# First attention layer: scores of the next batch directly behind the values, normalised rows on ACT, another order of projections and banks

## The chip, the cores and the metric

The kernel runs on one core of one Trainium2 chip. The metric is the device time of one execution in microseconds, as the median of several runs. The profile comes from one further execution that the hardware profiler recorded. The engines are PE (TensorE: matmuls; PEld is its weight load), DVE (VectorE), ACT (ScalarE), POOL (GpSimd) and SP (SyncE, which here only issues DMAs). Each engine works through its own instructions in order; semaphores order them against each other. PSUM has eight banks, which PE alone fills with products and DVE and ACT read.

## What is computed

x is 32 batches of 128 rows of 128 features; the context is 32 x 77 x 128. Two layers follow each other, each a cross-attention and a feed-forward part, with a layer norm ahead of each part and a residual behind it. The change touches only the attention of the first layer:

```python
x = x + _L0_xattn_ref(_layernorm(x, axis=-1), ctx_1024, ctx_1024, L0_xattn_Wq, ..., L0_xattn_Wo, mask_BxSxS2_ik0)
...
Q = (q @ Wq).reshape(b, ql, N_HEAD, QK_DIM)      # 16 heads of 64
K = (k @ Wk).reshape(b, kl, N_HEAD, QK_DIM)
V = (v @ Wv).reshape(b, kl, N_HEAD, V_DIM)
Q, K = (rope(Q), rope(K))
attn = jnp.einsum('bqhd,bkhd->bhqk', Q / scale, K)
attn = jnp.where(mask[:, None, :, :] == 0, -INF, attn)
attn = jax.nn.softmax(attn, axis=-1)
out = jnp.einsum('bhqk,bkhd->bqhd', attn, V).reshape(b, ql, N_HEAD * V_DIM)
return out @ Wo
```

## The kernel before

Every engine's program of this layer is a loop over 32 slots, one for each batch b, written out in full; a pair p = b // 2 of batches shares one set of queries, and j = b % 2 tells the even from the odd slot. Keys are projected for quads of four batches in eight tasks `("K", n)`, values in five tiles of 128 context rows for eight batches (`("V", u, half)`), queries of the next pair in four tasks `("Q", p + 1, k)`, and the turned normalised rows of the pair after it in one task `("X", p + 2)`.

In a slot PE does this for batch b: `all_scores` (L1274: 32 float32 products that make the scores with the keys as rows, in three banks `ps` and one bank `pa`; L1278: 16 bfloat16 products, the folds, that add mask and row maximum from the tile `fold`), `values` (L1296: probabilities times values), `turn_out` (L1307: the normalised output is transposed), `out_projection` (L1316). For batch b + 1 it does `score_maxima` (L1223 lays the mask into `ps`, L1232 adds bfloat16 scores with the queries as rows; DVE takes the row maxima of them at L911 and writes them into `am`) and `turn_maxima` (L1244: `am` is transposed into `ps[0]`; ACT copies it into `fold` in `fold_in`, L1057). Projections are split products of three fp32r matmuls each (L1172 to L1174). PE transposes `xhat` at L1164.

DVE ropes the query and key tasks out of their bank (L845, L848 for queries; L855, L858 for keys; the second one frees the bank), POOL finishes the rope (L741, L742, L753, L755), ACT casts the result to bfloat16 for the maxima (`cast_queries` L1045, `cast_keys` L1053). ACT also takes the exponents (`exps`, L1062 for the group in `pa`, L1067 for those in `ps`), copies the values out of their bank (`values_in`, L1040) and the transposed output (`turned_out`, L1073). DVE normalises the output (`normalise`, L917 to L924), adds the residual (L929), and makes the rows of the pair p + 2: `statistics`, `masks` (L801, L802) and `normalised_rows` (L817: a 128x2 scale; L819: two 128x128 steps), which write `xhat`.

The projections, the turned rows and one group of scores share the two banks `pa[0]` and `pa[1]`. `pa_tasks` lists them in PE's order and `TASK` deals them out in turn: each task takes the bank that the last but one had, and PE waits until that one's reader has freed it. `TASK` sets no order itself; PE's order is the one in which `slot` is written. `VALUE_SLOT` and `KEYS` say which slot projects what. In all the text below, a slot of kind A is b = 4q, B is 4q + 1, C is 4q + 2 and D is 4q + 3. The layer's scores begin at 30 us and its last slots end at about 440 us. In layer 1, L1788 is an ACT `Identity` with a bias, which stands in one loop with exponents (L1812).

Of the kernel before, what the change touches and what calls it, by code (L numbers as in the profile page):

```python
# [403 lines left out]
def layer0_attention(nc, ctx, t):  # L404
# [64 lines left out]
    setup = sem("setup")  # L469
    stats_ready, rstd_ready, xhat_ready = sem("stats_ready"), sem("rstd_ready"), sem("xhat_ready")  # L470
# [14 lines left out]
    VALUE_SLOT = {8 * o + s: VT * o + i for o in range(B // 8) for i, s in enumerate((-3, 0 if o == 0 else -1, 1, 3, 4))  # L485
                  if 8 * o + s >= 0}
# [3 lines left out]
    KEYS, LATE_KEYS = {0: range(4, 8), 1: range(8, 11), 2: range(14, 16)}, {1: range(11, 14)}  # L490
    for q in range(1, B // 4 - 1):
        n = 8 + 8 * q
        KEYS[4 * q], KEYS[4 * q + 1], LATE_KEYS[4 * q + 1] = range(n, n + 2), range(n + 2, n + 5), range(n + 5, n + 7)
        KEYS[4 * q + 2] = range(n + 7, n + 8)

    def middle_keys(b):

        return KEYS[0][:2] if b == 0 else ()

    def even_keys(b):  # L500

        return KEYS.get(b, ())[2 if b == 0 else 0:]

    def odd_keys(b):

        return KEYS.get(b, ())[:2], KEYS.get(b, ())[2:]

    def late_keys(b):

        return LATE_KEYS.get(b, ())  # L510

    def pa_tasks():

        yield from ([("X", 0)] + [("Q", 0, k) for k in range(4)] + [("V", 0, 0)] + [("K", n) for n in range(4)]
                    + [("V", 0, 1), ("C",), ("X", 1)])
        for b in range(B):
            p, u = b // 2, VALUE_SLOT.get(b)
            values = [] if u is None else [("V", u, 0), ("V", u, 1)]
            tasks = lambda ns: [("K", n) for n in ns]
            queries = [("Q", p + 1, k) for k in range(4)] if p + 1 < PAIRS else []  # L520
            if b < B - 2:
                yield "S", b
            if b % 2 == 0:
                yield from (queries[:2] + tasks(middle_keys(b)) + queries[2:3] + tasks(even_keys(b)[:-1]) + queries[3:] + values
                            + tasks(even_keys(b)[-1:]))
                continue
            ahead, behind = odd_keys(b)
            rows = [("X", p + 2)] if p + 2 < PAIRS else []
            if ahead:
                yield from tasks(ahead) + rows + tasks(behind) + values + tasks(late_keys(b))  # L530
            else:
                yield from values[:1] + rows + values[1:]
# [1883 lines left out]
```

## Time and profile before

| | us |
|---|---|
| median of 3 runs | 718.12 |
| the runs | 717.88, 718.12, 720.57 |
| the profiled execution | 719.26 |
| its span, first to last instruction | 716.7 |

| engine | busy us | share of the span |
|---|---|---|
| PE | 680.4 | 95% |
| PEld | 569.8 | 80% |
| DVE | 556.9 | 78% |
| POOL | 432.1 | 60% |
| ACT | 388.7 | 54% |

The page gives the share of busy time of each engine, the granted clock of PE (0.995 of full speed over the span, so the higher of its two levels, 2.4 GHz, nearly throughout), and the instructions by group. PE's matmuls are pipelined: a row of a single one shows some 0.2 to 0.5 us, while the next begins long before that ends. So the time that a matmul costs is the distance from its start to the next start, and a short wait can hide within the duration of the one before it without a gap.

### The profile page before, as it was taken

The numbers are of one execution on the slowest core, as the hardware profiler recorded it, in microseconds if no ns is written. First come the engines' busy times: TensorE is split into PE (matmuls) and PEld (weight loads), VectorE is DVE, ScalarE is ACT, GpSimd is POOL, SyncE is SP. The second block draws the span as 40 slices with busy tenths as digits, with TensorE's granted clock in tenths as the row PEclk, the third lists the DMA queues.
The fourth block names the chain that finished last, engine by engine and source line by source line (L and its number), as shares of the span: only waits on it lengthen the run. The fifth ranks groups of instructions, "written<-read, shape, count | busy, mean of one in ns | idle before, by whom it ended". The sixth has DMA issues, their size and how long they took to land.

```text
span 716.7 us, 23519 instructions
## 1 busy us (share of the span) xinstructions
PE 680.4 (95%) x9268; PEld 569.8 (80%) x9273; DVE 556.9 (78%) x1635; ACT 388.7 (54%) x846; POOL 432.1 (60%) x558
## 2 busy tenths in 40 slices
PE   8999999999999999999999989999999999998875
PEld 6788888888888888889888878788888888875544
DVE  5887787697687698688687655787878887778996
ACT  2443553543544544445345444566766766766896
POOL 3597586487396388378477523455555646632775
PEclk9999999999999999999999999999999999998999
DMA  9511011101101101101100120000000000000011
GB/s 263 132 34 37 13 48 45 33 5 46 37 26 45 36 2 45 36 26 36 36 22 15 32 79 7 11 7 7 12 5 4 9 4 9 0 2 1 24 45 52
DMA packets 26766, 23.82 MB, mean 33 GB/s; under 512 B 7148, under 2 KB 23356, under 8 KB 26680
## 3 DMA queue, kind: packets, MB, share of 16 engines
q1 hardware_dynamic: 25864, 22.25, 11.1%
q8 instruction: 62, 1.02, 0.6%
q10 hardware_dynamic: 816, 0.36, 0.2%
q14 instruction: 24, 0.20, 0.1%
HBM read 10.25 MB, written 2.10 MB: 17 GB/s over the span
## 4 chain that ended last, share of the span: by engine, by line
PE 70%; DVE 17%; POOL 5%; issue 4%; ACT 3%; DMA 1%; SPq 0%; ACTq 0%; DVEq 0%
PE bank L1274 7%; PE bank L1316 6%; PE bank L1942 6%; PE bank L1172 5%; PE bank L1296 4%; PE bank L1975 4%; PE bank L1278 4%; PE bank L1307 3%; PE bank L1173 3%; PE bank L1174 3%; DVE a_am L911 3%; PE bank L1960 2%; DVE f_h_max L2192 2%; PE bank L1223 2%; PE bank L1232 2%
## 5 line engine op out<-in xcount | busy, mean ns | idle before, releaser
L741 POOL TENSOR_TENSOR a_turned<-a_turned,a_rope 128x512 f32<-128x512 f32 x63 | 81.7, 1297 | 55.7 <-DVE a_turned L848 55.7
L742 POOL TENSOR_TENSOR a_qr<-a_straight,a_turned 128x512 f32<-128x512 f32 x64 | 81.6, 1276 | 4.9
L845 DVE TENSOR_TENSOR a_straight<-bank,a_rope 128x512 f32<-128x512 f32 x63 | 43.0, 683 | 52.5 <-PE bank L1174 51.4
L1045 ACT CAST a_qb<-a_qr 128x512 bf16<-128x512 f32 x64 | 39.8, 622 | 65.9 <-POOL a_qr L742 65.9
L1296 PE MATMUL bank<-a_vs,a_probs 77*64 77x65 f32 x2048 | 66.8, 222 | 0.0
L1296 PEld LDWEIGHTS bank<-a_vs,a_probs 77*64 77x64 f32 x2048 | 62.6, 137 | 3.3
L753 POOL TENSOR_TENSOR a_k_turned<-a_k_turned,a_rope 128x308 f32<-128x308 f32 x61 | 48.4, 793 | 24.3 <-DVE a_k_turned L858 23.6
L1316 PE MATMUL bank<-a_wo,a_oTn 128*128 128x128 f32 x512 | 62.6, 275 | 0.2 <-ACT a_oTn L1073 0.2
L1316 PEld LDWEIGHTS bank<-a_wo,a_oTn 128*128 128x128 f32 x512 | 60.5, 192 | 1.2 <-ACT a_oTn L1073 0.5
L911 DVE TENSOR_REDUCE a_am<-bank 128x6 bf16<-128x462 f32 (+1 forms) x96 | 49.9, 576 | 12.1 <-PE bank L1232 12.0
L1274 PE MATMUL bank<-a_qr,a_kr 64*77 64x128 f32 x960 | 59.2, 273 | 0.0
L1057 ACT COPY a_fold<-bank 112x128 bf16<-112x128 bf16 x32 | 8.5, 266 | 92.4 <-PE bank L1244 92.4
L1067 ACT ACTIVATE a_probs<-bank 77x512 f32<-77x512 f32 x98 | 52.8, 593 | 7.5 <-PE bank L1258 7.5
L1274 PEld LDWEIGHTS bank<-a_qr,a_kr 64*77 64x77 f32 x960 | 52.3, 144 | 5.2 <-issue 5.1
L755 POOL TENSOR_TENSOR a_kr<-a_k_straight,a_k_turned 128x308 f32<-128x308 f32 x62 | 52.0, 840 | 4.8
L848 DVE STREAM_SHUFFLE a_turned<-bank 128x512 f32<-128x512 f32 x63 | 46.3, 735 | 0.0
L1674 DVE TENSOR_REDUCE a_max_m<-bank 128x8 f32<-128x512 f32 x64 | 41.1, 685 | 5.0 <-PE bank L1923 4.6
L1812 ACT ACTIVATE a_qr<-bank 128x512 f32<-128x512 f32 (+1 forms) x96 | 43.8, 536 | 1.0 <-PE bank L1960 1.0
L729 POOL TENSOR_TENSOR a_rstd<-a_var,minus_half 128x2 f32<-128x2 f32 x16 | 11.3, 707 | 51.1 <-DVE a_var L812 51.0
L1073 ACT COPY a_oTn<-bank 128x512 f32<-128x512 f32 x64 | 34.5, 589 | 13.4 <-PE bank L1307 12.8
L1172 PE MATMUL bank<-a_xT_hi,a_wq_hi 128*128 128x256 f32 x128 | 39.9, 312 | 1.3 <-DVE a_wq_lo L939 1.1
L1599 POOL TENSOR_TENSOR a_kr<-a_k_straight,a_blocks 128x128 f32<-128x128 f32 x32 | 12.8, 400 | 46.4 <-ACT a_k_straight L1794 46.4
(282 smaller groups left out, 1984.8 us busy)
## 6 DMA issues: line engine op xcount, KB each, us to landing
a_vs<-a_stage SPq DMA_DIRECT2D x16, 312.8 KB
out<-x_all SPq DMA_DIRECT2D x16, 128.0 KB, 1.8
x_all<-in_x_dram SPq DMA_DIRECT2D x7, 256.0 KB, 6.3
a_vs<-a_stage SPq DMA_DIRECT2D x4, 308.8 KB
a_mask_in<-in_mask SPq DMA_DIRECT2D x16, 77.0 KB, 5.7
a_wv<-in_ctx SPq DMA_DIRECT2D x16, 77.0 KB
a_ctx_in<-in_ctx SPq DMA_DIRECT2D x8, 128.0 KB
a_vs<-a_stage SPq DMA_DIRECT2D x4, 211.2 KB
```

The source lines that it names most:

```text
L741: steps.link(nc.gpsimd.tensor_tensor(tv, tv, rope[:, 1:2, :].broadcast_to([128, 4, S]), ALU.mult))
L742: nc.gpsimd.tensor_tensor(qr[P][:, 2 * k:2 * k + 2, :, :].rearrange("p t j s -> p (t j) s"), sv, tv, ALU.subtract if made else ALU.add).th ...
L753: steps.link(nc.gpsimd.tensor_tensor(tv, tv, rope[:, 3:4, 0:KL].broadcast_to([128, 4, KL]), ALU.mult))
L755: nc.gpsimd.tensor_tensor(kr[q % 2][:, lo:hi, first:end, :].rearrange("p i j s -> p i (j s)"), view(k_straight[n % 3]), view(k_turned[n % ...
L848: nc.vector.stream_shuffle(turned[k % 3][:], pv, mask=[lane ^ 1 for lane in range(32)]).then_inc(a_free[TASK["Q", p, k][0]], 1)
L911: nc.vector.tensor_reduce(rows, ps[bk][:, 0:n * KL].rearrange("p (h k) -> p h k", k=KL), AX, ALU.max).then_inc(s_free[bk], 1)
L1067: nc.scalar.activation(probs[:, 4 * g:4 * g + 4, :], ps[ST_BANK[g]][0:KL, :].rearrange("p (h s) -> p h s", s=S), ACT.Exp).then_inc(s_free[ ...
L1172: nc.tensor.matmul(out, lhs_hi, rhs_hi, start=True, stop=False)
L1274: nc.tensor.matmul(banks[g][0:KL, i * S:(i + 1) * S], kr[b // 4 % 2][e:e + 64, h // 2, b % 4, :], qr[P][e:e + 64, h // 2, j, :], start=i = ...
L1296: last = nc.tensor.matmul(po[r][rows, VW * i:VW * (i + 1)], probs[:, PROBS_SLOT[h], rows], vs[b % RING][:, h, :], start=True, stop=True)
L1316: last = nc.tensor.matmul(po[2][:, 0:D], oTn[:, i, :], wo[:, i, :], start=i == 0, stop=i == TILES - 1)
L1812: nc.scalar.activation(probs[:, 4 * g:4 * g + n, :], SCORES[g].rearrange("p (t s) -> p t s", s=S), ACT.Exp).then_inc(s_free[g], 1)
```

## The change

- The scores of batch b + 1 (the L1274 part, without the folds) are written directly behind `values(b)`, ahead of `turn_maxima(b + 1)` and `turn_out(b)`; the slot of b + 1 then begins with the folds (`all_folds`). For batches 0 to 29.
- `turn_maxima` writes a bank `pa` (a new task `("T", b)`) in place of `ps[0]`.
- `turned_out(b)` on ACT stands at the end of slot b in place of the next slot's start or middle; ACT's exponents of a slot are no longer divided by it.
- `normalised_rows` of pairs 2 and up is four ACT steps in the even slot in place of three DVE steps in the odd one: two centre the rows, two scale them. The scale is made on POOL (one 128x2 product behind the power). What it needs of the mask comes from `mask_in` itself, with two DVE steps ahead of the statistics.
- PE's order of the projections and `pa_tasks` change: one key task stands directly behind the folds in A, B and C (`lead`), two in B; the first value tile stands in the middle of the slot between keys. `VALUE_SLOT` moves tile 0 of eight batches from slot 8o - 3 to 8o - 1, and tile 4 from 8o + 4 to 8o + 5.
- `score_maxima` lays the mask before it waits for the keys' cast, and waits for the queries' casts too.
- SP loads the mask of pair 2 before the later loads, and each further one a slot earlier.

The core of the diff:

```diff
-    VALUE_SLOT = {8 * o + s: VT * o + i for o in range(B // 8) for i, s in enumerate((-3, 0 if o == 0 else -1, 1, 3, 4))
-                  if 8 * o + s >= 0}
+    VALUE_SLOT = {0: (1,), **{8 * o + 1: (VT * o + 2,) for o in range(B // 8)}, **{8 * o + 3: (VT * o + 3,) for o in range(B // 8)},
+                  **{8 * o + 5: (VT * o + 4,) for o in range(B // 8)},
+                  **{8 * o - 1: (VT * o, VT * o + 1) for o in range(1, B // 8)}}
...
     def statistics(p):
+            if p > 1:
+                dve.wait_ge(xhat_ready, p)
+                dve.wait_ge(masks_in[p % 2], 16 * (p // 2) + 16)
+                steps.link(nc.vector.tensor_reduce(kept[p % 2][:], mask_in[p % 2][:], AX, ALU.max, apply_absolute_value=True))
+                steps.did(nc.vector.tensor_scalar(kept[p % 2][:], kept[p % 2][:], 0.5, -1.0, ALU.is_ge, ALU.mult))
...
     def scalar(act, second):
+        def normalised_rows(p):
+            act.wait_ge(rstd_ready, p + 1)
+            for j in range(2):
+                nc.scalar.activation(xhat[:, j, :], x[:, 2 * p + j, :], ACT.Identity, bias=mv[p % 2][:, j, 0:1],
+                                     scale=-1.0).then_inc(rows_centred, 1)
+            for j in range(2):
+                act.wait_ge(rows_centred, 2 * (p - 2) + j + 1)
+                last = nc.scalar.activation(xhat[:, j, :], xhat[:, j, :], ACT.Identity, scale=scale[:, j:j + 1])
+            last.then_inc(xhat_ready, 1)
...
+                exps(b, (3, 0, 1, 2))
+                if j == 0:
+                    if more_pre(p):
+                        normalised_rows(p + 2)
+                    cast_keys(b + 1)
...
+                fold_in(b + 1)
+                if b + 1 < B - 2:
+                    turned_out(b, 0)
+                    turned_out(b, 1)
...
         def score_maxima(b, P, j):
-            pe.wait_ge(cast_done, b + 1)
+            pe.wait_ge(masks_made, b // 2 + 1)
             for m in (2, 0, 1):
...
+            pe.wait_ge(cast_done, b + 1)
+            pe.wait_ge(queries_cast, Q_GROUPS * (b // 2 + 1))
...
         def turn_maxima(b, P, j):
...
+            if b < B - 2:
+                nc.tensor.transpose(empty(pe, ("T", b))[:].bitcast(BF16)[0:FOLD, 0:S], am[P][:, j, :],
+                                    t["identb"][:]).then_inc(a_full[TASK["T", b][0]], 1)
+                return
...
+        def all_folds(b):
+            pe.wait_ge(a_free[TASK["T", b][0]], TASK["T", b][1] + 1)
...
             elif j == 0:
-                all_scores(b, P, j)
+                all_folds(b)
+                for n in lead:
+                    project_keys(n)
+                project_queries(p + 1, (0,))
+                if not first:
+                    out_projection(b - 1)
+                project_queries(p + 1, (1,))
...
                 for r in range(3):
                     values(b, P, j, r)
+                all_scores(b + 1, P, 1)
                 turn_maxima(b + 1, P, 1)
-                if u is not None:
-                    project_values(u, 0)
-                    project_values(u, 1)
-                for n in even_keys(b)[-1:]:
-                    project_keys(n)
+                turn_out(b)
```

PE from the end of the values of batch 1 (slot B) into the next slot, before: the maxima are turned, a value tile and three key tasks follow, then `turn_out(1)` and the scores with their folds.

```order
L1296 MATMUL bank<-a_vs,a_probs 64x65 x7
L1244 MATMUL bank<-identb,a_am 112x128 [waits a0_s_free0,a0_s_free2,a0_s_free1]
L1172 MATMUL bank<-a_wv_hi,a_ctxT_hi 128x512 [waits a0_a_free1]
...
L1174 MATMUL bank<-a_ctxT_hi,a_wk_lo 128x308
L1307 MATMUL bank<-ident,a_out_n 128x128 [waits a0_normalised]
L1307 MATMUL bank<-ident,a_out_n 128x128 x5
L1307 MATMUL bank<-ident,a_out_n 128x128 [waits a0_normalised]
L1307 MATMUL bank<-ident,a_out_n 128x128
L1274 MATMUL bank<-a_qr,a_kr 77x128 [waits a0_s_free1,a0_s_free2]
```

The same place now:

```order
L1342 MATMUL bank<-a_vs,a_probs 64x65 x7
L1316 MATMUL bank<-a_qr,a_kr 77x128 [waits a0_s_free1,a0_s_free2]
L1316 MATMUL bank<-a_qr,a_kr 77x128 x7
L1316 MATMUL bank<-a_qr,a_kr 77x128 [waits a0_a_free1,a0_s_free0]
L1316 MATMUL bank<-a_qr,a_kr 77x128 x7
L1283 MATMUL bank<-identb,a_am 112x128 [waits a0_s_free0,a0_a_free0,a0_s_free2,a0_s_free1]
L1353 MATMUL bank<-ident,a_out_n 128x128 [waits a0_normalised]
L1353 MATMUL bank<-ident,a_out_n 128x128 x5
L1353 MATMUL bank<-ident,a_out_n 128x128 [waits a0_normalised]
L1353 MATMUL bank<-ident,a_out_n 128x128
L1324 MATMUL bank<-a_fold,a_fold_w 77x128 [waits a0_a_free0]
```

The scores have moved ahead of the turned maxima and of `turn_out`, the value and key tasks have left this place, and the folds alone stand behind `turn_out`.

PE in the middle of slot B (batch 1), now: keys, two value halves, a key task and the turned rows follow `out_projection`, with the bank that each waits for.

```order
L1362 MATMUL bank<-a_wo,a_oTn 128x128 x3
L1208 MATMUL bank<-a_ctxT_hi,a_wk_hi 128x308 [waits a0_a_free1]
...
L1208 MATMUL bank<-a_wv_hi,a_ctxT_hi 128x512 [waits a0_a_free0,a0_a_free1]
...
L1208 MATMUL bank<-a_wv_hi,a_ctxT_hi 128x512 [waits a0_a_free1]
...
L1208 MATMUL bank<-a_ctxT_hi,a_wk_hi 128x308 [waits a0_a_free1,a0_a_free0]
...
L1200 MATMUL bank<-ident,a_xhat 128x128 [waits a0_contexts_in0,a0_a_free1,a0_xhat_ready]
```

Before, this place held the turned rows and one key task behind `out_projection`, and the value halves came behind the turned maxima.

ACT in the even slot C (batch 2), before:

```order
L1073 COPY a_oTn<-bank 128x512 [waits a0_turned_full] x2
L1053 CAST a_kb<-a_kr 128x616 [waits a0_a_free1,a0_a_free0,a0_k_roped]
L1062 ACTIVATE a_probs<-bank 77x512 [waits a0_a_full0]
L1067 ACTIVATE a_probs<-bank 77x512 [waits a0_s_full0]
L1067 ACTIVATE a_probs<-bank 77x512 [waits a0_s_full1]
L1067 ACTIVATE a_probs<-bank 77x512 [waits a0_s_full2]
L1045 CAST a_qb<-a_qr 128x512 [waits a0_roped]
```

And now:

```order
L1103 COPY a_oTn<-bank 128x512 [waits a0_turned_full] x2
L1092 ACTIVATE a_probs<-bank 77x512 [waits a0_a_full1]
L1097 ACTIVATE a_probs<-bank 77x512 [waits a0_s_full0]
L1097 ACTIVATE a_probs<-bank 77x512 [waits a0_s_full1]
L1097 ACTIVATE a_probs<-bank 77x512 [waits a0_s_full2]
L1043 ACTIVATE a_xhat<-x_all,a_mv 128x128 [waits a0_rstd_ready]
L1043 ACTIVATE a_xhat<-x_all,a_mv 128x128
L1047 ACTIVATE a_xhat<-a_xhat,a_scale 128x128 [waits a0_rows_centred] x2
L1080 CAST a_kb<-a_kr 128x616 [waits a0_a_free1,a0_a_free0,a0_k_roped]
L1072 CAST a_qb<-a_qr 128x512 [waits a0_roped]
```

The four steps of the rows have come in behind the exponents, and the cast of the keys, for which `score_maxima` waits, has moved from ahead of the exponents to behind the rows.

## Rows read from the trace of the kernel before

**Rows 1.** The steady stretch: bounds; length; busy PE, PEld, DVE, ACT, POOL; clock; DMA.
```profile
48.00:420.00 372.00, 362.62 (x5142) 316.87 (x5139) 283.62 (x737) 174.23 (x350) 244.20 (x242) 1.00 0.12 34
```

**Rows 2.** PE's waits, 48 to 420 us: waiting, releaser, total, times, longest.
```profile
PE bank L1164 <- DVE a_k_turned L858: 2.0, 3, 0.7
PE bank L1244 <- DVE a_am L911: 1.7, 4, 0.4
PE bank L1307 <- DVE a_out_n L918: 1.4, 6, 0.3
```

**Rows 3.** Timeline of PE at four waits: start, length, instruction, idle time before.
```profile
155.89 1.95 PE L1316 MATMUL bank<-a_wo,a_oTn 128*128 128x128 f32 x16
158.52 0.41 PE L1164 MATMUL bank<-ident,a_xhat 128*128 128x128 f32 x2 [0.68 <-DVE a_k_turned L858]
...
216.58 0.40 PE L1174 MATMUL bank<-a_wv_hi,a_ctxT_lo 128*128 128x512 f32 x1
217.04 0.38 PE L1172 MATMUL bank<-a_ctxT_hi,a_wk_hi 128*128 128x308 f32 x1
...
217.40 0.31 PE L1174 MATMUL bank<-a_ctxT_hi,a_wk_lo 128*128 128x308 f32 x1
217.75 0.38 PE L1172 MATMUL bank<-a_ctxT_hi,a_wk_hi 128*128 128x308 f32 x1
...
241.18 0.40 PE L1174 MATMUL bank<-a_wv_hi,a_ctxT_lo 128*128 128x512 f32 x1
241.83 1.09 PE L1307 MATMUL bank<-ident,a_out_n 128*128 128x128 f32 x8 [0.26 <-DVE a_out_n L918]
```

**Rows 4.** Timeline of PE where it waits for nothing: its price by starts.
```profile
216.11 0.40 PE L1172 MATMUL bank<-a_wv_hi,a_ctxT_hi 128*128 128x512 f32 x1
...
221.13 1.09 PE L1278 MATMUL bank<-a_fold,a_fold_w 112*77 112x128 bf16 x16
222.02 0.36 PE L1172 MATMUL bank<-a_xT_hi,a_wq_hi 128*128 128x256 f32 x1
...
223.54 1.95 PE L1316 MATMUL bank<-a_wo,a_oTn 128*128 128x128 f32 x16
225.24 0.36 PE L1172 MATMUL bank<-a_xT_hi,a_wq_hi 128*128 128x256 f32 x1
```

**Rows 5.** Timeline of ACT and PE around `turn_out` and the next folds.
```profile
242.52 1.07 ACT L1073 COPY a_oTn<-bank 128x512 f32<-128x512 f32 x2 [0.33 <-PE bank L1307]
243.48 0.72 ACT L1053 CAST a_kb<-a_kr 128x616 bf16<-128x616 f32 x1
245.21 0.59 ACT L1062 ACTIVATE a_probs<-bank 77x512 f32<-77x512 f32 x1 [1.01 <-PE bank L1278]
245.71 1.55 ACT L1067 ACTIVATE a_probs<-bank 77x512 f32<-77x512 f32 x3
...
244.76 1.09 PE L1278 MATMUL bank<-a_fold,a_fold_w 112*77 112x128 bf16 x16
```

**Rows 6.** DVE and ACT groups: count, busy us, mean ns, idle; then one timeline row.
```profile
L819 DVE SCALAR_TENSOR_TENSOR a_xhat<-x_all,a_mv,a_scale 128x128 f32<-128x128 f32 x28 | 28.6, 1060 | 0.5
L817 DVE SCALAR_TENSOR_TENSOR a_scale<-a_kept,a_rstd 128x2 f32<-128x2 f32 x13 | 10.7, 823 | 0.4
L1788 ACT ACTIVATE a_k_straight<-bank,a_bk 128x154 f32<-128x154 f32 x16 | 6.2, 389 | 7.6 <-PE bank L1894 7.6
...
26.18 0.61 DVE L819 SCALAR_TENSOR_TENSOR a_xhat<-x_all,a_mv,a_scale 128x128 f32<-128x128 f32 x2
```

**Rows 7.** Timeline: how soon DVE and ACT free a bank.
```profile
216.31 1.29 ACT L1040 COPY a_stage<-bank 128x512 f32<-128x512 f32 x2 [0.56 <-PE bank L1174]
...
218.15 0.50 DVE L858 STREAM_SHUFFLE a_k_turned<-bank 128x308 f32<-128x308 f32 x1
```

**Rows 8.** Timeline of PE and ACT at the layer's first scores.
```profile
30.00 1.98 PE L1274 MATMUL bank<-a_qr,a_kr 64*77 64x128 f32 x32
...
30.10 0.27 ACT L1057 COPY a_fold<-bank 112x128 bf16<-112x128 bf16 x1 [0.45 <-PE bank L1244]
```

More of the change, by code:

```diff
@@ L527, in pa_tasks @@
[L527 to L530, printed above, removed]
-            else:
-                yield from values[:1] + rows + values[1:]
+            p = b // 2
+            lead, second, middle, late = ([("K", n) for n in some] for some in keys_at(b))
+            first_half, second_half = ([("V", u, half) for u in ahead_values(b)] for half in range(2))
@@ new lines, in pa_tasks @@
+            later_first, later_second = ([("V", u, half) for u in later_values(b)] for half in range(2))
+            if b % 2 == 0:
+                queries = [("Q", p + 1, k) for k in range(4)] if p + 1 < PAIRS else []
+                if b == 0:
+                    yield from (queries[:2] + first_half + middle[:1] + second_half + middle[1:] + queries[2:3] + late[:1]
+                                + queries[3:] + late[1:])
+                else:
+                    yield from lead + queries
+            else:
+                rows = [("X", p + 2)] if p + 2 < PAIRS else []
+                yield from (lead + second + middle[:1] + first_half + second_half + middle[1:] + later_first + rows
+                            + later_second + late)
@@ L766, in slot @@
         def slot(b, p, P, j, more):
+            lead, second_keys, middle, late = keys_at(b)
             if j == 0:
@@ L780, in slot @@
                     rope_turn(p + 1, 1 - P, 3)
-                for n in even_keys(b)[-1:]:
+                for n in late[1:]:
                     rope_keys(n)
             else:
-                ahead, behind = odd_keys(b)
-                for n in (*ahead, *behind, *late_keys(b)):
+                for n in (*lead, *second_keys, *middle, *late):
                     rope_keys(n)
@@ L963, in slot @@
             first = b == 0
+            lead, second_keys, middle, late = keys_at(b)
             if j == 0 and last_pair(p):
@@ L1005, in slot @@
                     next(second)
+                if more_pre(p) and lead:
+                    split_turned(("X", p + 2))
                 if more:
                     maxima(b + 1, 1 - P, 0)
-                if more_pre(p) and not ahead:
+                if more_pre(p) and not lead:
                     split_turned(("X", p + 2))
+                for n in late:
+                    rope_keys(n)
                 normalise(b)
@@ L1132, in slot @@
[L1132 to L1145 removed]
+                exps(b, (2, 3))
@@ L1351, in tensor @@
         idle_products(6)
+        all_scores(0, 0, 0)
         turn_maxima(0, 0, 0)
         def slot(b, p, P, j, more):
-            first, u = b == 0, VALUE_SLOT.get(b)
+            first = b == 0
+            lead, second_keys, middle, late = keys_at(b)
             if j == 0 and last_pair(p):
```

243 lines of the change are left out of this document (128 added, 115 removed).

## The prediction

> **What bounds the kernel now.** I read the busy times first, then the steady stretch of the first layer, then PE's waits in it, then the starts of single matmuls. The page gives PE 95% busy over the span; in the stretch from 48 to 420 us it is 362.6 of 372.0 us, DVE 283.6, POOL 244.2, ACT 174.2 [rows 1]. PE bounds the stretch. The number of its products stays the same, so the change can only take away waits of PE, or make new ones. Nothing behind the layer's last slots is touched.
>
> PE's idle time there is 372.0 - 362.6 = 9.4 us, and three of its releasers are DVE: the rows of the pair ahead (2.0 us), the row maxima (1.7), the normalised output (1.4) [rows 2]. The reader should not stop at these. A matmul's record reaches over part of the wait behind it, so I compare starts [rows 3]. Between the start of the last value product and `turn_out` lie 0.65 us where 0.23 is the price of that product (0.47 for two, from 216.11 to 216.58 [rows 3, 4]): 0.42 lost, of which the view shows 0.26. From a value tile to a key task it is 0.46 in place of 0.23, with no idle time shown, and from a key task to the next 0.35, of which I take 0.14 as the price. `out_projection` takes 1.70 us [rows 4] where nothing holds it; before the turned rows it took 2.63 (155.89 to 158.52), some 0.85 too much.
>
> Counted over the slots by their order: about 17 waits at value and key tasks for a bank, 0.22 each and all hidden (3.7 us), and some 16 others that hide about 0.15 beside what is shown (2.4). **All of PE's waits there come to 9.4 + 3.7 + 2.4 = 15.5 us.** That is the most that perfect cover could give in this stretch, 2% of the kernel.
>
> **The rows move from DVE to ACT.** DVE gives up L819 and L817, in one pair of batches 2 x 1.06 + 0.82 = 2.94 us [rows 6], and the reduction of `kept` moves rather than goes. It gains a 128x2 step. The work is in slots B and D, just ahead of where PE waits for it; afterwards it is in A and C, on ACT. That ends the wait of the turned rows (2.0 us shown), and makes key tasks and maxima in B be served sooner. The two L819 take 0.61 us together at 26.18 [rows 6], where POOL is idle, and 1.06 each on the mean beside POOL.
>
> The Trainium skill (page "SBUF — State Buffer", section "SBUF: two separate sides") says that a VectorE operation with two SBUF inputs and a GpSimd operation that reads SBUF shut each other out for a whole instruction, and that ScalarE waits for neither. The trace agrees on the first half with 0.61 against 2 x 1.06. It also speaks against a small part of this change: the new 128x2 step reads and writes SBUF in a form that would take the same lock, so that beside POOL it may wait out one POOL step. No row here shows that step.
>
> On ACT the rows cost four 128x128 steps. The nearest row is L1788, 128x154 with a bias, 0.39 us [rows 6]; below it lies about 0.3, above it 0.5 with the wait between centring and scaling. I take 0.45, so 1.8 us a pair, 1.2 to 2.4. ACT is 47% busy, so it has the room; whether it stands in anybody's way is a matter of place. In A and C the keys' cast now stands behind them. ACT starts `turned_out` 0.69 us after `turn_out` began and is done 0.96 later (241.83, 242.52, 243.48 [rows 3, 5]), so it is free 1.65 us behind that start. `turn_out` takes 0.9 to 1.0; so the first exponent can start 0.7 us into the slot, and the four take 2.05 (245.21 to 247.26 [rows 5]). The rows end at 2.8 + 1.8 = 4.6, the cast (0.6 to 0.7) at 5.3. PE needs it behind folds 0.9, key 0.5, three query tasks of 0.75, `out_projection` 1.7 and the mask's 0.65: at 6.0. Cover of 0.7 us, so I cost this at nothing; each microsecond beyond that would cost 14, once for each pair.
>
> POOL gets one more 128x2 step behind the power (about 0.8 us, an estimate from L817, the same shape on DVE [rows 6]); its 244 of 372 us hide that, and the rows are wanted only at 2.8 into the slot.
>
> **The scores move behind the values.** Two waits get cover. The scores stand 1.9 us long between the values and `turn_out`, so DVE's normalising is done when `turn_out` starts: the seven waits of 0.4 (2.8 us) go. The maxima are wanted for the scores' banks at the same place as before, so their 0.48 us waits go only as far as DVE is earlier; it is, by the 2.9 us above. Against that, the folds lose the scores as cover for `fold_in`: it starts 0.10 us behind the scores' start and takes 0.27 at the first batch [rows 8], and `turn_out` with its 0.9 us covers it in every slot but the first. There nothing does: **+0.7 us** once (one bank wait with it, 0.4 to 1.0).
>
> There is a second effect, of changes between kinds of matmul: a split product's first matmul is dearer by 0.08 behind another kind (the first two of a key task take 0.36, from 217.04 to 217.40, where 0.14 is the price of one), and a score behind a projection alike. The order has about one such change less in a slot. 28 slots by 0.08 would be -2.2; the passage from `turn_out` to the folds is in no row and may cost as much. I take **-1.0**, bounds -3 and +2.
>
> **The other order of projections.** A bank is free about 1.1 us after the last start of a key task (217.40 to 218.65, less 0.14 [rows 3, 7]), and a value half about 0.9 us after its end (ACT's 0.59 and some 0.25 ahead of it). In B the order is now key, value half, value half, key, turned rows, and every task takes the bank of the last but one. The second value half wants the bank of the key two places ahead, with only a half of 0.70 us between (0.47 for two products, so 0.70 for three [rows 3, 4]): about 0.45 lost. The turned rows want the bank of that half with only a key of 0.44 between: about 0.35 lost. So 0.8 us in each of seven slots B: **5.6 us of waits stay or are new**, 3 to 7. In A, C and D I find each bank freed in time: the query tasks are spread over `out_projection`. In A, B and C a second task directly behind the folds wants the bank of the first exponent. That is done at 0.7 + 0.6 = 1.3 us, and wanted at 0.9 + 0.44 = 1.35. I cost it at nothing, with 0.3 as the far end, in 21 slots.
>
> In slot 0, V and K tasks now stand among the first queries and wait for DVE's 1.25 us a query; by the same working 1.75 us of waits against 1.5 before: **+0.2**. In the last slots one wait for DVE stays, which no scores cover (0.7), and small ones of ACT: **1.0 stays**. Values in place, masks and the later loads: the values' tile 0 is made about a slot ahead of its use, over 10 us, and the masks come sooner than before. Both at nothing.
>
> **The sum.** 15.5 - 5.6 - 1.0 = 8.9 us of waits gone, 1.0 for the kinds, less 0.7 and 0.2: 9.0. My list surely misses a few small waits; I take 0.5 off for them. The profiled execution of 719.26 becomes 710.8. It lies 1.14 above the median of 718.12, which carries over: **709.6 us**.
>
> **The rivals.**
> 1. *The wait moves to the exponents.* The task behind the lead key waits 0.3 us in 21 slots, since ACT now does `turned_out` ahead of the exponents: 6.3 us back, 715.9. For it speaks that my cover is 0.05 us. Against it, that the exponent's 0.59 us is measured, and that `turned_out` stood ahead of the exponents in even slots before too, with no idle time of PE behind it.
> 2. *The rows on ACT hold up the maxima.* If the four steps came late (the statistics late on DVE, a step of 0.8 us and not 0.45, or a change of function between exponent and identity), the keys' cast would end beyond 6.0 us and PE would stand at `score_maxima` in 14 even slots. It decides from 0.7 us; at 1.7 us late it costs 14, less the 8.5: 723.6. Against it: L1788, an identity among exponents, takes 0.39 [rows 6].
> 3. *Nearly all waits go.* If DVE frees the banks in B quicker since nothing is queued ahead, and the order of kinds gives its 3: 15.5 - 2 + 3 less 0.9 is 15.6, so 702.5.
> 4. *Nothing happens*, since DVE is behind all along and the waits only change their names: 718. Against it, DVE's 283.6 of 372 fall by some 35.
>
> **How the numbers follow.** Forecast (705 to 713.5) 0.60; rival 1 and mixtures with it (713.5 to 717) 0.20; rival 3 0.10; rival 4 0.04; rival 2 0.06. The range 703.5 to 716.5 leaves out 2 in 10. A measurement can tell 0.5% from no change, so 714.5 and 721.7 are the bounds: faster takes the forecast, rival 3 and a part of rival 1, 0.77; same 0.17; slower 0.06.
>
> **What would show it.** In the profile after: PE 48 to 410 us with 4 to 6 us idle and not 9.4; no wait at the turned rows except in B, where the releaser is ACT's value copy and not DVE; `turn_out` directly behind the turned maxima; value half to value half in B 0.7 us apart rather than 0.23; the cast of the keys 0.5 us or more ahead of the scores of `score_maxima`. Wrong would be: gaps behind the lead key, released by the exponents (rival 1), or ahead of L1270 by ACT's cast (rival 2), or DVE's busy time not falling by some 2.5 us a pair.

## The result, and the profile after

The changed kernel takes 714.83 us (median of 20 runs, 713.07 to 716.88), the kernel before 718.71 in the same sessions (20 runs, 717.54 to 720.57). The ratio is 0.9941, 95% interval 0.9931 to 0.9952: 4.2 us faster by the ratio (3.9 by the two medians), where 8.5 were forecast. The sign and the range held, the size did not. The profiled execution took 713.36 us, its span is 711.6.

Page of the kernel after: span, busy times, and the engines of the chain that ended last.

```profile
span 711.6 us, 23628 instructions
PE 678.8 (95%) x9273; PEld 571.7 (80%) x9273; DVE 521.4 (73%) x1607; ACT 401.5 (56%) x902; POOL 435.8 (61%) x572
...
PE 83%; DVE 9%; issue 3%; ACT 3%; DMA 1%; POOL 0%; SPq 0%; ACTq 0%; DVEq 0%
```

On the page of before DVE was busy for 556.9 us and ACT for 388.7, and the chain was 70% PE and 17% DVE. DVE has lost 35 us, and half of its share of the chain.

First the stretch from 48 to 410 us (bounds; length; busy PE, PEld, DVE, ACT, POOL; clock; DMA), then PE's waits in it (waiting line, releaser, total, times, longest). In this kernel L1208 is the first product of a projection, L1200 the transpose of the rows.

```profile
48.00:410.00 362.00, 355.94 (x5070) 315.66 (x5067) 247.09 (x705) 185.27 (x401) 247.59 (x255) 1.00 0.11 31
...
PE bank L1208 <- DVE a_k_turned L874: 3.2, 8, 0.5
PE bank L1200 <- ACT a_stage L1067: 2.4, 7, 0.3
PE bank L1208 <- ACT a_probs L1092: 0.5, 1, 0.5
```

PE is idle for 6.1 us where it was 9.4 [rows 1]; up to 414 us, which is as far into the layer as 420 us in the kernel before, it is 6.1 us too. The waits for the maxima and for the normalised output are gone, and so is one that [rows 2] does not list, `score_maxima` for the cast of the keys:

```profile
PE bank L1223 <- ACT a_kb L1053: 1.8, 3, 0.9
```

The turned rows still wait, 2.4 us in seven slots where it was 2.0 in three, now for ACT's copy in place of DVE; and DVE's turned keys still release 3.2 us (2.0 and 1.1 before). What is left are banks that the order of projections asks for early. By starts, in the way of [rows 3], I count some 12 us of waits up to 414 us against the 15.5 of before: only 3 to 4 us of waits went.

The same eight slots, by the windows between the masks of `score_maxima`: before from 133.90 us, after from 134.40 us.

```profile
133.90:237.44 103.54, 101.54 (x1438) 88.92 (x1437) 81.20 (x212) 48.56 (x99) 68.79 (x68) 1.00 0.12 33
```
```profile
134.40:236.70 102.30, 100.83 (x1438) 89.32 (x1437) 70.80 (x204) 52.34 (x115) 69.79 (x72) 1.00 0.12 34
```

1.24 us less for eight slots; 10.4 us less on DVE (2.6 a pair) for 3.8 more on ACT. Between the scores of `score_maxima` of slots 4 and 28 there are 306.2 us in place of 310.5 (-4.3); the three slots behind that give 2.5 more, and the first four, to my surprise, take 1.9 away: 56.7 in place of 54.8. In both of these 0.7 us is work that has only changed its place: one value half (three matmuls) stood in slot 28 and stands among the first slots now.

**Slot B.** Timeline of PE in the B slot at 157 us (start, length, instruction, idle time before).

```profile
157.77 0.30 PE L1210 MATMUL bank<-a_ctxT_hi,a_wk_lo 128*128 128x308 f32 x1
...
158.37 0.39 PE L1210 MATMUL bank<-a_wv_hi,a_ctxT_lo 128*128 128x512 f32 x1
159.15 0.47 PE L1208 MATMUL bank<-a_wv_hi,a_ctxT_hi 128*128 128x512 f32 x1 [0.39 <-DVE a_k_turned L874]
...
160.21 0.30 PE L1210 MATMUL bank<-a_ctxT_hi,a_wk_lo 128*128 128x308 f32 x1
160.85 0.41 PE L1200 MATMUL bank<-ident,a_xhat 128*128 128x128 f32 x2 [0.34 <-ACT a_stage L1067]
...
162.82 0.30 PE L1210 MATMUL bank<-a_ctxT_hi,a_wk_lo 128*128 128x308 f32 x1
163.10 0.38 PE L1208 MATMUL bank<-a_ctxT_hi,a_wk_hi 128*128 128x308 f32 x1
```

158.37 to 159.15 is 0.78 where 0.23 is the price of the product: 0.55 lost for the middle key's bank. 160.21 to 160.85 is 0.64 where 0.14 is the price: 0.50 lost for the value half's. 162.82 to 163.10 loses another 0.14, with no idle time shown, at the second late key. Together 1.2 us in each of seven slots B (the last of them lacks the 0.14).

**The task behind the lead key.** In slot 8, as in every slot with a lead key: the first exponent on ACT, then PE's last matmul of the lead key and the first of the task behind it.

```profile
142.04 0.60 ACT L1092 ACTIVATE a_probs<-bank 77x512 f32<-77x512 f32 x1
142.55 0.30 PE L1210 MATMUL bank<-a_ctxT_hi,a_wk_lo 128*128 128x308 f32 x1
142.79 0.36 PE L1208 MATMUL bank<-a_xT_hi,a_wq_hi 128*128 128x256 f32 x1
```

142.55 to 142.79 is 0.24 where 0.14 is the price: 0.10 lost, with no idle time shown. The exponent that frees the bank ends at 142.64, and PE starts 0.15 us later. In all 20 such slots from 51 us on PE's start lies 0.14 to 0.15 us behind the end of this exponent; in 19 of them 0.10 us is lost, in slot 1 0.62. That makes 2.5 us in all.

**The first slots.** PE at the first folds, at key task 7 of slot 0, at the second key task of slot 1 and at the first query task of slot 2.

```profile
32.07 1.09 PE L1324 MATMUL bank<-a_fold,a_fold_w 112*77 112x128 bf16 x16 [0.36 <-ACT a_fold L1084]
...
44.08 0.31 PE L1208 MATMUL bank<-a_ctxT_hi,a_wk_hi 128*128 128x154 f32 x1 [1.22 <-DVE a_k_turned L874]
...
51.77 0.38 PE L1208 MATMUL bank<-a_ctxT_hi,a_wk_hi 128*128 128x308 f32 x1 [0.46 <-ACT a_probs L1092]
...
67.78 0.36 PE L1208 MATMUL bank<-a_xT_hi,a_wq_hi 128*128 128x256 f32 x1 [0.48 <-DVE a_k_turned L874]
```

By starts they lose 0.55, 1.38, 0.62 and 0.64 us. Only the first was in the forecast's sum.

**ACT.** The rows and the keys' cast in an even slot; on PE the scores that want the cast start at 147.42.

```profile
142.53 1.57 ACT L1097 ACTIVATE a_probs<-bank 77x512 f32<-77x512 f32 x3
143.96 0.71 ACT L1043 ACTIVATE a_xhat<-x_all,a_mv 128x128 f32<-128x128 f32 x2
144.54 0.71 ACT L1047 ACTIVATE a_xhat<-a_xhat,a_scale 128x128 f32<-128x128 f32 x2
145.13 0.72 ACT L1080 CAST a_kb<-a_kr 128x616 bf16<-128x616 f32 x1
```

The four steps take 1.17 us, a little under the low end of what was taken, and the cast is done at 145.85, 1.57 us ahead of its reader.

### The profile page after: what moved, and what is told of

It reads as the page before. It is cut to its first block, busy times and chain, and to the rows that moved or that the text cites. A ratio compares the mean times of both kernels' runs of the same rounds, so it can differ in the third digit from the quotient of the medians.

```text
span 711.6 us, 23628 instructions
## 1 busy us (share of the span) xinstructions
PE 678.8 (95%) x9273; PEld 571.7 (80%) x9273; DVE 521.4 (73%) x1607; ACT 401.5 (56%) x902; POOL 435.8 (61%) x572
## 4 chain that ended last, share of the span: by engine, by line
PE 83%; DVE 9%; issue 3%; ACT 3%; DMA 1%; POOL 0%; SPq 0%; ACTq 0%; DVEq 0%
PE bank L1342 9%; PE bank L1362 8%; PE bank L1316 8%; PE bank L1208 6%; PE bank L2006 6%; PE bank L2039 4%; PE bank L1209 4%; PE bank L1210 4%; PE bank L1353 4%; PE bank L1324 4%; PE bank L1259 2%; PE bank L2024 2%; PE bank L1270 2%; DVE f_h_max L2256 2%; PE bank L1980 1%
## 5 line engine op out<-in xcount | busy, mean ns | idle before, releaser
L871 DVE TENSOR_TENSOR a_k_straight<-bank,a_rope 128x308 f32<-128x308 f32 x61 | 28.9, 473 | 43.2 <-PE bank L1210 42.2
L762 POOL TENSOR_TENSOR a_kr<-a_k_straight,a_k_turned 128x308 f32<-128x308 f32 x62 | 52.3, 844 | 4.8
L945 DVE TENSOR_TENSOR x_all<-bank,x_all 128x128 f32<-128x128 f32 x32 | 9.3, 292 | 50.1 <-PE bank L1362 50.0
L1208 PE MATMUL bank<-a_xT_hi,a_wq_hi 128*128 128x256 f32 x128 | 40.1, 313 | 1.6 <-DVE a_wq_lo L955 0.9
```

The source lines that it names most:

```text
L762: nc.gpsimd.tensor_tensor(kr[q % 2][:, lo:hi, first:end, :].rearrange("p i j s -> p i (j s)"), view(k_straight[n % 3]), view(k_turned[n % ...
L1208: nc.tensor.matmul(out, lhs_hi, rhs_hi, start=True, stop=False)
```

## The experiments

Each run was timed beside the kernel before on the same chip. E0 is the changed kernel itself; the edits are made in it. A slot's length is from the scores of its `score_maxima` to the next ones.

**E0, the changed kernel again (two sessions).**

> The changed kernel as it is, beside the others on the same chip. 714.8 us as measured before (its single runs lay between 713.1 and 716.9).

Measured: 714.76 us (713.38 to 717.75, 6 runs), ratio 0.9943 [0.9923, 0.9963].

**E1, a cover for the value half in B.** Half of `out_projection` stands between the value halves, and DVE serves the middle key ahead of the residual.

```diff
-                out_projection(b - 1)
+                out_projection(b - 1, range(4) if lead else range(TILES))
                 for n in middle[:1]:
                     project_keys(n)
...
                         project_values(u, 0)
+                    out_projection(b - 1, range(4, TILES))
+                    for u in ahead_values(b):
                         project_values(u, 1)
```

> The changed kernel with one edit in slot B: the out projection is cut into two halves and its second half stands between the two value halves, and DVE ropes the middle key ahead of the residual. The bank order of the tasks stays. Theory (the gain is missing at banks that are asked for too soon): the wait of the second value half for the middle key, 0.55 us in each of seven slots B, goes, the one of the turned rows for ACT (0.50) stays: 3.8 us less than the changed kernel, 711.0. Rival (PE's own work has become dearer by the new order, or the waits only move to the next task): within 1 us of the changed kernel.

Measured: 711.51 us (710.60 to 714.29), ratio 0.9903 [0.9886, 0.9921], 3.3 below E0. PE at the second value half and the turned rows of a slot B (the cut above shows PE's part of the edit alone):

```profile
158.42 1.05 PE L1364 MATMUL bank<-a_wo,a_oTn 128*128 128x128 f32 x8
159.23 0.48 PE L1210 MATMUL bank<-a_wv_hi,a_ctxT_hi 128*128 128x512 f32 x1
...
160.94 0.41 PE L1202 MATMUL bank<-ident,a_xhat 128*128 128x128 f32 x2 [0.34 <-ACT a_stage L1069]
```

The wait at the value half is gone, the one at the turned rows stays. Slots B take 14.10 us in place of 14.51: 2.9 over seven, a little under seven times 0.55, since the first value half now starts 0.28 us behind the key and not 0.14. So the wait for the bank in B is a real price and not an artefact of the records. Whether PE's cover or DVE's earlier key took it away the run doesn't say, since both moved.

**E2, a cover for the three waits of the first slots.** Key task 7 goes behind the values of slot 0; in slot 1 the exponents go ahead of a cast of queries; in slot 2 key task 15 goes behind the second query task. The cut shows the first of the three moves.

```diff
                 project_queries(p + 1, (3,))
-                for n in late[1:]:
-                    project_keys(n)
                 for r in range(3):
                     values(b, P, j, r)
+                for n in late[1:]:
+                    project_keys(n)
```

> The changed kernel with three edits in its first slots: the last key task of slot 0 behind the values; the cast of the second query task of pair 1 behind slot 1's exponents; key 15 behind the second query task of slot 2. Theory: the three waits that slots 0 to 2 have newly (1.38, 0.62 and 0.64 us) go, but DVE is full in slot 0 and keeps a part: 2.3 us less than the changed kernel, 712.5. Rival (the layer's start is bound by DVE's work and not by the order): less than 0.8 us.

Measured: 712.75 us (712.37 to 713.75, 5 runs), ratio 0.9919 [0.9906, 0.9931]. Slot 1 fell from 17.79 to 16.3 us. Slot 2 rose from 13.90 to 14.47: key task 15 waits for nothing at its new place, but the query task behind it now wants the bank of the one before, with only the key between. One of the three moves was a loss.

**E3, both.**

> The edits of both kernels, the cut out projection and the three of the start. Theory: the gains add, 6.1 us less than the changed kernel, 708.7. Rival: they do not add, since one engine (DVE) is behind in both; 711 or more.

Measured: 709.37 us (709.15 to 709.54, 4 runs), ratio 0.9868 [0.9853, 0.9882]. The gains add (5.4 below E0, against 3.3 and 2.0). The loss in slot 2 shows again:

```profile
68.18 0.30 PE L1212 MATMUL bank<-a_ctxT_hi,a_wk_lo 128*128 128x308 f32 x1
69.50 0.39 PE L1210 MATMUL bank<-a_xT_hi,a_wq_hi 128*128 128x256 f32 x1 [1.01 <-DVE a_turned L864]
```

**E4, the rows back on DVE.** ACT's four steps go; DVE makes the rows in the odd slots with two `scalar_tensor_tensor`. The scale has the other sign in the changed kernel, so from the third pair on the rows come out negated; the work is the same.

```diff
                     masks(p + 2, P)
+                    rows_here(p + 2)
...
-                    if more_pre(p):
-                        normalised_rows(p + 2)
                     cast_keys(b + 1)
```

> The changed kernel with the rows back on DVE: two 128x128 steps in the odd slots behind the masks, as before the change; ACT's four steps are gone, POOL still makes the scale. Theory: DVE gets 2.1 us of work ahead of the residual and the middle key in B, where the second value half already waits for that key; seven slots B get about 1.2 us longer, D hides it: 8 us more than the changed kernel, 723. Rival (DVE has enough air after the scores have moved, the rows on ACT bring nothing): within 1 us.

Measured: 715.69 us (715.15 to 719.53, 10 runs), ratio 0.9961 [0.9946, 0.9977]. The theory that DVE has no room for the rows in B fell. PE's waits from 48 to 410 us:

```profile
PE bank L1214 <- DVE a_k_turned L881: 4.2, 5, 1.7
PE bank L1206 <- ACT a_stage L1075: 2.4, 7, 0.3
PE bank L1214 <- ACT a_stage L1075: 2.0, 3, 0.7
```

The turned rows wait for the same value copy as in E0 and not for DVE. The second value half loses 0.83 in place of 0.55, slots B take 14.80, and the first one has a wait of 1.7 (in a profile whose clock fell at 46 us). Seven of the ten runs lie at 715.2 to 715.8, with a granted clock of 0.995 to 0.998; against the lowest group of the changed kernel's runs (713.3, see E8), which were taken in other sessions, the rows on ACT are worth some 2 us, an estimate with which 7 x 0.29 agrees.

**E5, the scores back behind `turn_out`.**

```diff
                     values(b, P, j, r)
-                all_scores(b + 1, P, 1)
                 turn_maxima(b + 1, P, 1)
                 turn_out(b)
+                all_scores(b + 1, P, 1)
```

This is the even slot; the odd one is changed alike.

> The changed kernel with the scores of the next batch behind turn_out and not behind the values, all else alike. Theory: the scores' 1.9 us are the cover of the normalising, which ends 1.2 us behind the values in D and 2 to 3 us in A, B and C; 40 us more than the changed kernel, 755. Rival (the normalising is done early enough, the place of the scores only changes the kinds of matmul): within 3 us.

Measured: 772.11 us (768.83 to 773.65, 5 runs), ratio 1.0755 [1.0737, 1.0773]. PE's waits in its first layer:

```profile
PE bank L1353 <- DVE a_out_n L934: 37.1, 29, 1.6
PE bank L1208 <- DVE a_k_turned L874: 3.4, 8, 0.7
```

1.28 us at each of 29 `turn_out`. In the kernel before value and key tasks stood in that gap and left 0.4 [rows 3]; in the new order these stand ahead of the values, and the scores alone cover DVE's normalising. The direction was right. Of the 57 us, 37 are this wait as the view shows it, and some 43 by starts. A further part is the clock: in the profile it stood at 0.50 in seven stretches between 45 and 438 us (the first 6.9 us long, the others 3.4 to 3.5), where the kernel after has none. In E0's profile such a fall of 6.8 us made slot 1 longer by 3.1 (see E8), so 27 us of it would cost some 13, an estimate; some of it overlaps the waits.

**E6 and E7, more work on ACT.** Four or eight further `Identity` steps of 128x128 between ACT's two pairs of row steps, into a tile that nobody reads.

```diff
+            for i in range(EXTRA):
+                nc.scalar.activation(act_spare[:, i, :], x[:, 2 * p, :], ACT.Identity, bias=mv[p % 2][:, 0, 0:1],
+                                     scale=-1.0).then_inc(spare_done, 1)
```

> The changed kernel with four more 128x128 identity steps on ACT between the centring and the scaling of each pair's rows, 1.2 us in each even slot; they write a tile that nobody reads. Theory: the cast of the keys ends 1.5 us ahead of PE's need (145.85 against 147.42 us in the trace), so nothing or at most 1 us. Rival (ACT's rows hold up the maxima already): 14 x 1.2 = 17 us more.

> As before with eight such steps, 2.4 us in each even slot. Theory: 0.9 us beyond the cover, times 14: 8 to 13 us more than the changed kernel. Rival (the cover is larger, since PE waits elsewhere anyway): under 4.

Measured: E6 715.38 us (714.98 to 715.90, 4 runs), ratio 0.9954 [0.9937, 0.9971]; E7 725.78 us (725.34 to 726.75, 4 runs), ratio 1.0099 [1.0082, 1.0116]. In E6 every slot from the fourth on is as long as in the kernel after, to 0.02 us. In E7 twelve even slots are longer by 0.81 each. Slot 0 is an exception in both: 15.20 and 16.25 us in place of 13.45. There ACT's copy of a value half stands behind the rows, PE waited 0.6 and 1.7 us for it, and the clock fell in both profiles near 40 us. In E7, 12 x 0.81 and 2.8 in slot 0 are the 12.4 us by which its span exceeds that of the kernel after. ACT's extra steps in E7 (the view ends among the eight), and a wait of PE in its first layer:

```profile
176.38 0.71 ACT L1045 ACTIVATE a_xhat<-x_all,a_mv 128x128 f32<-128x128 f32 x2
176.96 1.28 ACT L1049 ACTIVATE a_act_spare<-x_all,a_mv 128x128 f32<-128x128 f32 x4
```
```profile
PE bank L1276 <- ACT a_kb L1086: 9.0, 12, 0.8
```

Eight steps take some 2.4 us; less the 1.57 us of cover that leaves 0.83. Rival 2 is thus a true mechanism with its place (the keys' cast ahead of `score_maxima`) and its price, 0.81 an even slot. From slot 4 on the change lies 1.57 us on the safe side of it; for slot 0 the cover is smaller, and was not measured.

**E8, key task 7 alone, and E0 again.** The runs of the changed kernel come in three groups, and so do their mean granted clocks: eight of the 20 at 713.1 to 713.8 us (0.998, one each at 0.997 and 0.995), eight at 714.7 to 715.1 (0.994 or 0.995), four at 716.4 to 716.9 (0.990 to 0.992). The edit is the one shown under E2.

> The changed kernel again, beside the two that follow. Its executions so far fall into groups near 713.2, 715 and 716.8 us. My theory is that this scatter is TensorE's clock: after the wait of 1.4 us ahead of key task 7 in slot 0 the granted clock falls to its lower level in some executions, at other moments in each. So: median 714 to 716, lowest near 713.3, highest above 716, the mean granted clock lower in the longer ones.

> The changed kernel with one edit: in slot 0 key task 7 stands behind the values and no longer ahead of them, so that the wait of 1.4 us for its bank is covered. If the scatter is the clock that falls behind that wait, all executions lie within 1.2 us of each other, at 713.0 to 714.0, none near 715 or 717, and the profile shows the clock at 1.00 from 44 to 52 us; the wait itself brings little in the undisturbed executions, because DVE is what slots 0 and 1 are held by (e2_start lies only 0.6 below the lowest group with all its three waits mended). The rival, that the scatter comes from somewhere else (transfers, the second half of the program), keeps 715 and 717 in e8_key7 as well.

Measured: E0 714.26 us (713.46 to 716.84, 6 runs), ratio 0.9937 [0.9923, 0.9951]; E8 712.45 us (712.05 to 712.58, 4 runs), ratio 0.9910 [0.9896, 0.9924]. The window from 44 to 52 us (length; busy PE, PEld, DVE, ACT, POOL; the eighth figure is the clock) of the kernel after, of E0's profile, which took 716.70 us, and of E8:

```profile
44.00:52.00 8.00, 7.46 (x132) 6.96 (x133) 4.32 (x13) 2.72 (x7) 7.69 (x8) 1.00 0.02 6
```
```profile
44.00:52.00 8.00, 7.72 (x102) 7.47 (x102) 3.97 (x11) 0.00 (x0) 7.69 (x9) 0.57 0.03 8
```
```profile
44.00:52.00 8.00, 7.49 (x102) 6.75 (x99) 5.09 (x16) 3.89 (x9) 7.69 (x8) 1.00 0.01 3
```

And the 32 score products in it, of the kernel after and of E0 (busy, mean ns of one):

```profile
L1316 PE MATMUL bank<-a_qr,a_kr 64*77 64x128 f32 x32 | 2.0, 273 | 0.0
```
```profile
L1316 PE MATMUL bank<-a_qr,a_kr 64*77 64x128 f32 x32 | 3.1, 372 | 0.0
```

In E0's profile PE stood at key task 7 for 1.33 us, and from 44.7 us on the granted clock was 0.50 (1.2 GHz in place of 2.4) until 51.5 us. Slot 1 took 20.93 us in place of 17.79. In the profiles of E1 and E4 the fall lasted half as long (46.1 to 49.6 and 46.0 to 49.4 us), which would give a group between the other two; that the middle group of runs is this was not shown. The mean clock alone does not tell the groups apart: every profile, that of before too, has a fall in the second layer as well, 3.4 to 6.9 us long (654 to 661 us in the kernel after, 659 to 666 in the one before), and the profile of the kernel after has 0.995 with no fall in the first layer. With the wait covered the clock stays at 1.00 there and the scatter is gone: four runs within 0.53 us. All the kernels with key task 7 at its new place (E2, E3, E8, E9, E10) have 22 runs, none more than 1.4 us above the lowest of its kernel. That the wait sets off the fall is thus borne out by the move of one task, and not taken apart further. My side remark, that the wait itself costs little, was wrong: slot 1 is 0.97 us shorter, and E8 lies 0.9 below the lowest group of E0.

**E9 and E10, a better version.** E9 is E3 with `out_projection` in pieces of 3, 3 and 2 products in the slots B, the last one ahead of the turned rows, with DVE turning both middle keys ahead of the residual, and key task 15 behind `score_maxima` of slot 2. E10 puts that task behind `out_projection` of slot 2. The cut shows E9's pieces against E3; the first is `range(3)`.

```diff
-                    out_projection(b - 1, range(4, TILES))
+                    out_projection(b - 1, range(3, 6))
                     for u in ahead_values(b):
                         project_values(u, 1)
                 for n in middle[1:]:
                     project_keys(n)
+                if lead:
+                    out_projection(b - 1, range(6, TILES))
```

> e3_both with two more moves: out_projection in the slots B in three pieces (3, 3 and 2 products), the last one behind the second middle key, so that both waits for a bank have a piece ahead of them, with DVE turning both middle keys ahead of the residual; and in slot 2 key task 15 behind score_maxima rather than behind the second query task, where it made a wait of 1.2 us. Expected: the turned rows' wait of 0.50 falls to about 0.1 in seven slots B, the second value half's stays near 0.05: -2.8; the wait of 1.2 in slot 2 goes at least by half: -0.6 or more, unless DVE holds up slot 2. So 706.0, range 705.4 to 707.5. The rival: the banks are drained later since ACT's copy of the second value half or DVE's keys now meet the residual and the split, so that the wait moves on to later_values and the turned rows' split ahead of score_maxima: 708 to 710.

> e9_thirds with key task 15 at one more place: in slot 2 directly behind out_projection and ahead of the second query task, where its own bank (that of key task 14) and the one of the next task (that of the first query task) each have out_projection's 1.7 us as cover. In e9_thirds, where it stood behind score_maxima, the pieces in the slots B brought 0.23 us each (slot B 13.87 from 14.10 in e3_both), 1.6 us over seven, and slots 2 and 3 together took 27.16 in place of 26.00, because POOL and ACT had the key late and ACT's fold_in stands behind the cast of the keys. If that reading is right, slots 2 and 3 come to 25.2 (neither the wait of 1.2 of e3_both nor the 1.8 ahead of the folds of e9_thirds), and the whole to 707.2, range 706.6 to 708.0. If DVE is what holds up slot 2 wherever the key stands, they stay at 25.5 to 26.0 and the whole is 707.6 to 708.3. If key 15 is late again, 709.

Measured: E9 709.23 us (709.13 to 709.92, 4 runs), ratio 0.9868 [0.9853, 0.9882]; E10 707.41 us (706.94 to 707.46, 5 runs), ratio 0.9832 [0.9819, 0.9846]. In E9 the slots B fell to 13.87, but slot 3 had a new wait, ahead of the folds. PE, then ACT:

```profile
78.18 1.09 PE L1324 MATMUL bank<-a_fold,a_fold_w 112*77 112x128 bf16 x16 [1.64 <-ACT a_fold L1084]
```
```profile
76.74 0.71 ACT L1080 CAST a_kb<-a_kr 128x616 bf16<-128x616 f32 x1 [6.24 <-POOL a_kr L762]
77.35 0.61 ACT L1072 CAST a_qb<-a_qr 128x512 bf16<-128x512 f32 x1
77.87 0.26 ACT L1084 COPY a_fold<-bank 112x128 bf16<-112x128 bf16 x1
```

The cast of the keys waited for POOL's rope of the key task that now comes late, and the copy for the folds stood behind two casts in ACT's queue. In E10 slots 2 and 3 take 25.3 us together (27.2 in E9, 26.0 in E3), and PE's idle time from 48 to 410 us is down to 1.9 us:

```profile
48.00:410.00 362.00, 360.13 (x5157) 321.09 (x5157) 249.86 (x714) 188.29 (x407) 247.26 (x255) 1.00 0.11 32
```

E10 is 12 us below the kernel before and 7 below the changed one.

## Why the prediction was wrong, point by point

**What held.** PE was the bound, and waits were most of what there was to win. DVE's busy time fell by 2.6 us a pair (2.5 asked for). The waits for the maxima and the normalised output went; `turn_out` follows the turned maxima everywhere but at the last slot, where 0.67 us is shown against the 0.7 foreseen. The turned rows wait in B alone, for ACT's value copy. The first folds cost 0.55 (0.7), slot 0's two value halves and key 1.94 (1.75). ACT's cover was 1.57 us and not 0.7, mostly since the four steps took 1.17 and not 1.8. No wait of PE is put down to POOL's extra step. The Trainium skill (page "SBUF — State Buffer", section "SBUF: two separate sides") was drawn on for the new 128x2 step; it took 0.17 us at its shortest and 0.80 at its longest:

```profile
L820 DVE TENSOR_SCALAR a_kept<-a_kept x14: 169/472/803, 30.4 to 372.0; 128x2 f32<-128x2 f32 x14
```

The trace agrees with a lock against POOL, held for a whole instruction. Seven of the 14 took 0.17 us and have no step of POOL beside them. The other seven took 0.77 to 0.80, started 0.06 to 0.09 us after a step of POOL's L762, and ended within 0.06 us of its end: at 116.00 to 116.78 us, for one, with L762 from 115.91 to 116.75. No wait of PE came of it.

**Where it failed.** The idle time forecast for 48 to 410 us was 4 to 6, the profile has 6.1. The mechanism, waits for a bank two tasks back, was right; terms of its sum were mis-sized or left out.

1. *The waits in B.* Forecast 0.8 us a slot and 5.6 in all; measured 1.2 and 8.3, so 2.7 too little. The two waits that were named cost 0.55 and 0.50 where 0.45 and 0.35 stood, and the 0.14 at the second late key wasn't seen. E1 takes the first away and gives 2.9 back. In E10 the slots B are 0.64 us shorter each, 4.5 over seven: a good half. Cutting `out_projection` has a price of its own, such as 0.28 us ahead of the first value half in E9, where E0 has none.
2. *The first slots.* "+0.2" and "+0.7" stood for slot 0. The waits at key task 7 (1.38) and in slot 2 (0.64) were not in the sum: 2.0. I had worked out the general slot B and then treated slots 0 to 2, which have tasks of their own, as if they were alike. E8 gives 0.9 for the first of them.
3. *The exponents' bank.* Costed at nothing, with 0.05 us of cover. The cover is not there: 0.10 us is lost in 19 slots and 0.62 in slot 1, 2.5 in all. This is read from starts; no run took it away, and E10 has it still, at 0.10 in all 20.
4. *The clock.* No term stood for it. The lowest group of the 20 runs has a mean of 713.3, their median is 714.8: 1.5 us, which E8 and E2 do not have.

That is 8.7 us of misses against a gap of 4.3. The rest went the other way.

5. *The kinds of matmul.* Forecast -1.0. In the eight slots above, 103.54 - 3.5 of waits is 100.0 of work before, and 102.30 - 3.0 is 99.3 after, where 3.0 is 1.2 in two slots B and 0.10 in six others. So 0.7 for eight slots, some 2.5 for 28, and 1.5 more than was taken. Slots 2 to 29 in one piece, less the waits and the work that changed its place, give some 3, an estimate too. Why the work is cheaper no run took apart; the prediction's own count of changes, 28 by 0.08, gives 2.2.
6. *Taken off for nothing.* "1.0 stays" for the last slots was subtracted from 15.5, which was counted up to 420 us. These waits lie behind that, in both kernels (0.67 at 420.71 us before, at 415.52 after), so they were no part of it. The 0.5 for missed waits was taken off as well, though points 2 and 3 show far more than that.

```profile
420.71 1.09 PE L1307 MATMUL bank<-ident,a_out_n 128*128 128x128 f32 x8 [0.67 <-DVE a_out_n L918]
```

With these the misses come to 5.2 to 5.7 us, so 0.9 to 1.4 of the sum stays open. The last slots' gain of 2.5 us is 0.7 of moved work and over 1 us of waits that the kernel before had in slots 28 and 29, the longest for ACT's cast of the keys (0.52 shown at 416.65 us); the rest is point 5.

**The rivals.** Rivals 3 and 4 did not come. Rival 1 came at a third of its size, 0.10 us a slot in place of 0.3. E7 shows that rival 2 exists, 1.57 us away. Without the scores behind the values the new order loses 57 us (E5), which says what the order rests on and not what that one move is worth in the order before; the rows on ACT add about 2 us (E4). The other parts of the change, such as the mask ahead of the keys' cast and the earlier loads, were not tested one by one.

## What to carry to other kernels

When tasks take two banks in turn, write down for every task the time since the last start of the task two places ahead, and compare it with how long that bank takes to be drained (here 1.4 us for a key task); a piece of other work of PE between the two, like a third of `out_projection`, can take the wait away. Do not cost a cover of 0.05 us at nothing when 20 slots hang on it. Do this for the first and last slots by themselves, since they hold tasks and readers that no other slot has. And before an engine is given work, find the step behind it in its queue that somebody waits for, and how long before: that cover was 1.57 us from slot 4 on, and E6 and E7 stand on either side of it, while slot 0 had less.

## What was not expected of the hardware

One wait of PE of 1.4 us at 43 us, with PE busy for nearly all of the two microseconds before it, was followed in some executions by the lower granted clock (6.8 us of it in E0's profile, some 3.5 in those of E1 and E4) and in others by none; it turned a kernel whose parent scatters within 3.0 us into one with three groups of times over 3.8, and its median lies 1.5 us above the lowest group. Waits of 1.2 us at 69.5 in E3 and of 1.8 at 78 in E9 were followed by no such fall in their profiles. In E5, with a wait of 1.28 us on the mean in 29 slots, the clock fell in seven places. In E6, whose slot 0 is 15.2 us in place of 13.45, the clock fell earlier, to 0.79 in the window from 36 to 44 us. So a difference of medians of under 2 us between two such kernels says little until the groups of the runs are laid beside each other: E4 looked like 0.9 by the medians and is some 2 by the undisturbed groups. The mean granted clock helps in this but is not enough, as the fall in the second layer enters it too.

How long a small step of DVE takes can hang on POOL alone: the 128x2 step took 0.17 us by itself, and 0.77 to 0.80 where it started just behind a 128x308 step of POOL.
